# One pre-norm transformer layer on one core: the order of the attention matmuls inside a unit is changed

## What is computed

```python
x = hidden                                  # (B=4, S=512, D=512), fp32
qkv = layernorm(x) @ w_attn + b_attn        # 32 heads of 16 columns each
scores = q @ k.T / 16 + slope[h] * (j - i)  # ALiBi bias, causal
attn = softmax(scores) @ v
x = x + attn @ w_proj + b_proj
h = layernorm(x)
x = x + (silu(h @ w_gate.T) * (h @ w_up.T)) @ w_down.T   # 1376 inner columns
```

## Time and profile before

| | us |
|---|---|
| median of 3 runs | 922.75 (920.37 to 922.88) |
| the profiled execution, its own time | 921.12 |
| its span, first to last instruction | 919.4 |

### The profile page before, as it was taken

The page is one execution under the profiler, slowest core; times in us unless marked ns, Lnnn a source line. Parts: engine busy times, 40 slices in busy tenths (PEclk is TensorE's granted clock), DMA queues, the critical chain, the costliest instruction groups (busy, mean ns, idle before and its releaser), DMA issues. The chain is left out here.

```text
span 919.4 us, 13759 instructions
## 1 busy us (share of the span) xinstructions
PE 860.3 (94%) x5088; PEld 580.1 (63%) x5088; DVE 477.3 (52%) x931; ACT 364.1 (40%) x693; POOL 183.5 (20%) x337
## 2 busy tenths in 40 slices
PE   1999799999999999999998579999999999999998
PEld 1755355556555565555543268887888788878886
DVE  6586577766777667776773154443222322232223
ACT  4345455565556655565555233322111211111111
POOL 4223233342433324333342300000000000000000
PEclk9999899999999999999999879999999999999999
DMA  8764445655565455735461364203000310021001
GB/s 267 207 208 140 122 146 170 185 155 161 177 207 164 137 171 186 227 112 170 143 207 49 113 227 155 89 0 137 2 1 1 96 41 0 0 77 60 0 0 46
DMA packets 70562, 109.33 MB, mean 119 GB/s; under 512 B 13395, under 2 KB 38662, under 8 KB 70505
## 3 DMA queue, kind: packets, MB, share of 16 engines
q1 hardware_dynamic: 68457, 108.32, 37.5%
q10 hardware_dynamic: 2048, 0.27, 0.2%
HBM read 65.97 MB, written 42.32 MB: 118 GB/s over the span
## 5 line engine op out<-in xcount | busy, mean ns | idle before, releaser
L839 DVE TENSOR_REDUCE bm<-bank 128x3 f32<-128x384 f32 (+1 forms) x384 | 223.0, 596 | 118.8 <-PE bank L1045 114.7
L700 ACT ACTIVATE pt<-bank 128x512 f32<-128x512 f32 (+1 forms) x384 | 196.8, 528 | 168.4 <-PE bank L1067 162.9
L1067 PE MATMUL bank<-q_st,k_st 116*128 116x512 bf16 (+3 forms) x512 | 136.7, 309 | 18.0 <-DMA q_st<-mt 10.5
L1336 DVE TENSOR_TENSOR gu<-bank,silu 128x512 f32<-128x512 f32 x44 | 30.5, 692 | 220.2 <-issue 132.7
L1147 PE MATMUL bank<-fT_hi,wgu_hi 128*128 128x512 f32 x352 | 138.8, 394 | 5.5 <-DVE wgu_lo L1308 3.5
L1043 PE MATMUL bank<-k_st,q_st 97*128 97x512 bf16 (+3 forms) x512 | 141.6, 302 | 0.8 <-DMA q_st<-slopes_dram 0.6
L1147 PE MATMUL bank<-fT_lo,wgu_hi 128*128 128x512 f32 x352 | 138.4, 393 | 0.0
L1147 PE MATMUL bank<-fT_hi,wgu_lo 128*128 128x512 f32 x352 | 137.7, 391 | 0.0
L1067 PEld LDWEIGHTS bank<-q_st,k_st 116*128 116x128 bf16 x512 | 41.7, 98 | 131.0 <-ACT pt L700 72.1
L1045 PE MATMUL bank<-mask_qk,identb 128*128 128x128 bf16 x512 | 106.4, 220 | 0.0
L610 POOL TENSOR_SCALAR_AFFINE_SELECT pt<-pt 128x256 f32<-128x256 f32 x128 | 52.7, 412 | 213.1 <-ACT pt L700 213.1
(11 more groups left out here) (95 smaller groups left out, 1217.0 us busy)
## 6 DMA issues: line engine op xcount, KB each, us to landing
stack_dram<-part SPq DMA_DIRECT2D x32, 384.0 KB, 2.6
q_st<-stack_dram SPq DMA_DIRECT2D x32, 384.0 KB
k_st<-stack_dram SPq DMA_DIRECT2D x32, 384.0 KB
stack_dram<-part SPq DMA_DIRECT2D x32, 256.0 KB, 3.1
pv_dram<-weighed SPq DMA_DIRECT2D x32, 256.0 KB, 4.8
weighed<-pv_dram SPq DMA_DIRECT2D x17, 256.0 KB
xt<-x SPq DMA_DIRECT2D x16, 256.0 KB, 4.3
stack_dram<-part SPq DMA_DIRECT2D x32, 128.0 KB, 3.9
```

Of the source, the lines that this page charges most:

```text
L700: act.activation(pt[:, h % PT_RING, COL0[k]:COL0[k] + WIDE[k]], bank[3 + (3 * h + k) % 2][:, 0:WIDE[k]], ACT.Exp, scale=1.0 / HD).then_inc ...
L839: dve.tensor_reduce(bm[:, h % 4, BM_AT[k]:BM_AT[k] + BM_N[k]], bank[k][:, 0:BM_N[k] * P].rearrange("p (n q) -> p n q", q=P), AX.X, ALU.max ...
L1067: last = pe.matmul(bank[3 + u % 2][:, at:at + n], k_st[0:K_EXP, s, h % 4, t * P:(t + 1) * P], q_st[0:K_EXP, s, h % 4, t * P:S], start=True ...
L1336: dve.tensor_tensor(gu[:, f % 2, :], bank[5 + 2 * (f % 2)][:, :], silu[:, f % 2, :], ALU.mult).then_inc(gu_done, 1)
```

## The change

TensorE issues `scores(h + 8, k)` ahead of `shifted_scores(h, k)`. The eight projection matmuls of a head are issued as 4, 4 and 0 after the three units in place of 3, 3 and 2. The two tiles of unit 1 of `shifted_scores` swap places, the narrow one first; they are written to the same columns as before. All four tiles of `weigh_values` follow unit 1 of head 0. `transpose_maxima` moves from the end of head 1 to after its unit 0, `copy_maxima` on VectorE from head 2, after unit 0, to head 1, after unit 1, and `place_maxima` on ScalarE from the end of head 2 to the end of head 1. `copy_pv` on ScalarE moves from head 1, after the first exponential, to the end of head 0. No instruction is added or removed.

```diff
@@ scalar
-                    if i == 1 and c > 0:
-                        copy_pv(c - 1)
...
                     exponential(h, 2)
+                    if i == 0 and c > 0:
+                        copy_pv(c - 1)
+                    if i == 1 and c + 1 < CHUNKS:
+                        place_maxima(c + 1)
...
                     if i == 2:
-                        if c + 1 < CHUNKS:
-                            place_maxima(c + 1)
@@ vector
                     scored(0)
-                    if i == 2 and c + 1 < CHUNKS:
-                        copy_maxima(c + 1)
...
                     scored(1)
+                    if i == 1 and c + 1 < CHUNKS:
+                        copy_maxima(c + 1)
@@ tensor, shifted_scores
-                at = 0
-                for t in T_TILES[k]:
+                for t in T_TILES[k][::-1]:
                     n = S - t * P
+                    at = S - P if t == 3 else 0
                     last = pe.matmul(bank[3 + u % 2][:, at:at + n], ...
-                    at += n
@@ tensor, the loop over chunks and heads
                     for k in range(3):
+                        scores(h + AHEAD, k)
                         shifted_scores(h, k)
-                        scores(h + AHEAD, k)
-                        if i > 0:
-                            between(c, 8 * (i - 1) + 3 * k, 8 * (i - 1) + min(3 * k + 3, 8))
-                        if i == 0 and c > 0:
-                            if k == 1:
-                                weigh_values(c - 1, (0,))
-                            if k == 2:
-                                weigh_values(c - 1, (1, 3, 2))
+                        if i > 0 and k < 2:
+                            between(c, 8 * (i - 1) + 4 * k, 8 * (i - 1) + 4 * k + 4)
+                        if (i, k) == (0, 1) and c > 0:
+                            weigh_values(c - 1, (0, 1, 3, 2))
+                        if (i, k) == (1, 0) and c + 1 < CHUNKS:
+                            transpose_maxima(c + 1)
                         if (i, k) == (1, 0) and tokens_at(c, 1) is not None:
                             transpose_tokens(*tokens_at(c, 1))
-                    if i == 1 and c + 1 < CHUNKS:
-                        transpose_maxima(c + 1)
```

## The result

The kernel after takes 909.62 us (median of 4 runs, 907.91 to 910.15), the kernel before 921.99 beside it: a ratio of 0.9866, 95% interval 0.9844 to 0.9887. The direction was right; 897 was forecast with a range of 889 to 909, so the gain is half the forecast one. The profiled execution took 909.81 us with a span of 908.1, 11.3 less than before.

The account below looks back on a forecast made before the run. The prediction took TensorE, busy 94% of the span, to set the pace. Its terms, 11.7 + 7.0 + 7.5 + 1.5 - 2.2 = 25.5 us off 921.1, gave 895.6, and 897 as the median of runs; range 889 to 909.

Parts of the forecast that it names:

- Projections behind the mask: TensorE, entries from a mask into projections: 0.05 us lost at each of 9 a chunk, all saved in 26 chunks, 11.7 us.
- Weighing in one run: TensorE, head 0: one run and one entry fewer save 0.28 us a chunk; 7.0 us counted, bounds 2.8 to 10.
- Placement a head earlier: ScalarE's placement DMAs: leaving a head sooner cuts TensorE's 10.5 us of waits on placed maxima to 3, saving 7.5.
- the slow clock: TensorE at half clock after chunk 4's 4.4 us wait: the fall cost 2.9 us, half counted as saved, 1.5.
- The same issues take 1.15 us of ScalarE in either place ... The cost is nothing: ScalarE, the two placement DMA issues: as much slack in the new place, so moving them costs nothing.
- What is late next: Step listing four waits that come nearer in the new order, at masks, values, bank 6 and tokens: 2.2 us in sum.
- masks: Head 3 and the weighing behind it: GpSimd's zeroing comes 0 to 0.2 us late in 16 chunks; 0.5 us in all.
- values: ScalarE in four chunks: the second value tile is copied only after the last exponential, 0.2 us each, 0.8 in all.
- bank 6: transpose_maxima waits for copy_pv: needed at 5.1 us, ready at 4.8; 0.6 late without projections, covered by counting nothing there.
- tokens: Chunk 2's wait for VectorE's normalising grows 0.4 us; second transposes in 7 such chunks wait for VectorE, 0.5.
- the placement meets other traffic: Rival: placement DMAs land as late relative to their use, 7.5 + 1.5 us not saved: 906 us, chance 0.10.
- over 5 us at L1085 or L1053: Sign of a miss: new waits of that size on GpSimd (L1085) or ScalarE (L1053) would make the time too high.

Follow-up runs that it names:

- e5: The kernel after with unit 1's two tiles of shifted_scores back in their old order, 384 columns first and 128 last: 911.91 us.
- e9: The kernel after with the weighing split again, tile 0 after unit 1 and tiles 1, 3, 2 after unit 2 of head 0: 910.08 us.
- e2: The kernel before with only the maxima's transpose, copy and placement moved up by a head and copy_pv put at the end of head 0: 918.28 us.
- e1: The kernel before with only the order inside a unit changed (scores first, projections 4, 4, 0, narrow tile first): 925.26 us.
- e7: The kernel after without the two 384 KB stack loads of chunks 4 to 31, working on older stacks: 895.66 us.
- e8: The kernel before without the two 384 KB stack loads of chunks 4 to 31, as the control: 916.07 us.
- e11: The kernel after with the stack loads of chunks 4 to 31 cut to two of their four heads, half the bytes: 899.92 us.
- e10: The kernel after with K's second and third parts made during the weighing, and VectorE's P2 read and late group's first division moved later in head 3: 900.14 us.

## Why the prediction was wrong

- **Projections behind the mask: right.** 0.20 us a head where 0.15 was taken; e5 shows the cover, at 0.06 for one entry. Three entries at 0.06 are most of the 0.20. Full-array weight loads do hide behind a wide matmul, against the rule of the Trainium skill (TensorE: Matmul & The Clock Gate, Part 3) that the forecast weighed. In the rows of head 2 above, the second projection starts 0.45 us after a matmul of 512 columns. Taken 11.7, worth 15.6 in TensorE's rows.
- **Weighing in one run: near in the rows, wrong as a saving.** 0.24 a chunk for 0.28, but not as divided: the 0.09 at the entry that was left did not go, so one entry is 0.09 and the rest, 0.15, came from joining the runs, for which 0.10 was taken. The sum left out that unit 2's exponential goes behind the run, and K's second part behind that and `copy_pv`. e9: no net worth can be told from the times (910.08 against 909.62 and 911.84).
- **Placement a head earlier: mis-sized in what it replaced.** The 10.5 us went to 1.0 at L1067 (1.2 in the second timing), better than the 3 left. But at chunk 4, where the placement had been late, the stacks were: 2.9 us at the same place. In e2, which moves the placement alone, TensorE still waits 3.1 us for placed maxima there. Nor did the slow clock go; 1.5 us were counted, and 6.8 us of it are there as before.
- **"The same issues take 1.15 us of ScalarE in either place ... The cost is nothing": wrong, in the change's favour.** e1 shows them late in head 2 once the heads are shorter.
- **The step that failed is "What is late next"** with 2.2 us of new waits. It walked through TensorE's waits on engines (masks, values, bank 6, tokens), and these stayed small: L1053 on ScalarE 1.8 us, and L1084 on GpSimd 2.6, both times in the last weighing, where it was 1.8 before. It asked of no DMA whether its round trip still fits a chunk of 13.6 us, and gave K's parts and VectorE's two DMA waits no price. In chunks 8 to 27 that is 8.0 us (289.15 against 281.11), in chunks 0 to 7 4.8. A rival had the DMAs ("the placement meets other traffic"), but named the placement itself, and not the stacks or VectorE's loads. Nor did the signs set for a miss come, over 5 us at L1085 or L1053.
- **The sum without that step: near, by its heads.** e7 takes 895.66 us where 897 was forecast, but it leaves out loads that cost the kernel before 6 us as well. The fair pair is e8 and e7: 20.4 us, where 25 were forecast. In the clean chunks they differ by 16.2 us (297.3 to 281.1), above the 14.6 of the forecast heads and just the 16.4 of the measured ones. What is missing from 25 is mostly the placement's: e8 has lost the big wait of chunk 4 with the loads, and its L1067 waits 4.3 us for placed maxima where the kernel before waits 8.6 up to 475 us.
- **A slip without weight:** VectorE's 313.31 us in a loop shorter by 25.5 are 72% and not 71.

What stays open: e11 (fewer bytes, 10 us) and e10 (same bytes, earlier steps, 9.5 to 11.7) each give most of the 14 us of e7, so the two are not parts of a sum: either the bytes or the late step has to go. For chunks 8 to 27 the table above divides it. For chunks 0 to 7, where the traces of after and e7 differ by 4.8 us and each has its own falls of the clock, nothing here does. The profiled execution of e10 (907.14) is also slower than its median by 7 us. Some of that is a longer start: 58.4 us to chunk 0, then 6.6 us at the lower clock, with 4.81 us in head 1 of chunk 0 where the kernel after has 3.62.

## What to carry to other kernels

When TensorE's chunk gets shorter, list every chain that leaves the core and comes back within a chunk (part, store, load, use), and compare its length from the chunk's start with the new chunk, not with the old one: a step moved on ScalarE by 1.7 us cost more than the new order had won in some of the chunks it hit (13 took 15.47 us, 14.79 before). Look in each in-order queue for what is now ahead of the step that feeds a DMA, and put steps that wait for a DMA behind those that TensorE waits for. Parts of a change that shorten and parts that make room can't be priced alone: the order by itself lost 0.6%, the placement by itself won 0.3%, the two together won 1.1% (e9), and with the weighing joined 1.3%, which can't be told from 1.1.

## What the runs showed of the hardware

Three things were not expected. A weight load of 0.19 us in the profile needs only some 0.11 of cover, by an estimate from two rows: behind a mask of 0.06 the loss is 0.05, behind 384 columns none. The four-wide weighing loses 0.09 at its entry, and there 384 columns in front change nothing. And the two small placement DMAs take longer to land when they leave a head earlier: 1.6 to 6.3 us with a median of 2.1 before. The same summary of `mt`'s DMAs in the kernel after, from issue to landing:

```profile
DMA to landing us min/median/max: 1.6/3.1/6.7
```

The median is 3.1 us, as in e2, which moves the placement alone. Without the stack loads it is 2.6 (e7) against 2.0 (e8), so these loads explain about half of the difference. Only the longer lead hides it.
